# Down products of a gated feed-forward kernel moved: one wait for all chunks, and half of one group's products behind two steps of the next

## The reference

```python
x = x + L0_ffn(L0_cond(x))                  # shared + routed experts, top 2 of 8
# second layer
H     = x @ W.T                             # 256 -> 256
delta = ((x @ A_b.T) @ B_b.T) * s_b         # rank 16, one adapter for each batch row
h     = H + delta
gate  = gelu(fp8(h) @ fp8(w_gating[0]))     # 256 -> 1024, bf16 out
up    =      fp8(h) @ fp8(w_gating[1])      # 256 -> 1024, bf16 out
out   = fp8(gate * up) @ fp8(w_linear)      # 1024 -> 256
x = x + out
```

## Time and profile before

| | |
|---|---|
| median of 3 runs | 429.93 us |
| profiled execution, its own time | 429.1 us |
| its span | 427.3 us |
| TensorE busy | 412.4 us (97%) |
| VectorE, ScalarE, GpSimd busy | 309.2, 249.0, 193.2 us |
| groups 0 to 6 of the second layer | 289 to 411.7 us, some 17.5 us each |
| last group to the end | 411.7 to 427.3 us |

### The profile page before, as it was taken

The page is one execution under the profiler, slowest core; times in us unless marked ns, Lnnn a source line. Parts: engine busy times, 40 slices in busy tenths (PEclk is TensorE's granted clock), DMA queues, the critical chain, the costliest instruction groups (busy, mean ns, idle before and its releaser), DMA issues.

```text
span 427.3 us, 8683 instructions
## 1 busy us (share of the span) xinstructions
PE 412.4 (97%) x2954; PEld 331.7 (78%) x2954; DVE 309.2 (72%) x728; ACT 249.0 (58%) x552; POOL 193.2 (45%) x198
## 2 busy tenths in 40 slices
PE   7999789999999999999999999999999999999996
PEld 5567578887889999999999998885665756657553
DVE  5987898997987666666666663759587786777845
ACT  2987544667335665556655654438475494664854
POOL 2404229900544544455445403646575575754020
PEclk9999999999999999999999999999999999999999
DMA  8998300000145554655555622321143232322111
GB/s 250 381 388 297 99 0 2 1 2 0 54 128 179 167 161 144 181 160 158 165 159 176 152 87 74 88 74 51 52 134 95 66 111 74 113 87 61 49 51 50
DMA packets 37290, 50.44 MB, mean 118 GB/s; under 512 B 4504, under 2 KB 30496, under 8 KB 37248
## 3 DMA queue, kind: packets, MB, share of 16 engines
q1 hardware_dynamic: 29600, 31.53, 21.8%
q0 software_dynamic: 6512, 17.71, 15.7%
q10 hardware_dynamic: 1136, 0.65, 0.6%
HBM read 32.18 MB, written 17.69 MB: 117 GB/s over the span
## 4 chain that ended last, share of the span: by engine, by line
PE 81%; ACT 8%; DVE 7%; issue 2%; DMA 2%; POOL 0%; DVEq 0%; ACTq 0%; POOLq 0%
PE bank L1132 16%; PE bank L1134 16%; PE bank L1133 15%; PE bank L1408 13%; PE bank L1423 6%; PE bank L1294 4%; ACT xtr L468 2%; PE bank L1333 2%; PE bank L1332 2%; PE bank L1314 2%; PE bank L1374 2%; ACT xtT L482 2%; PE bank L1222 1%; DVE hsf L761 1%; DMA pick<-in_pick 1%
## 5 line engine op out<-in xcount | busy, mean ns | idle before, releaser
L403 POOL DMA_INDIRECT xg<-kept,perm x71 | 68.1, 959 | 91.2 <-PE bank L1294 54.9
L1408 PE MATMUL bank<-h,wg 128*128 128x512 fp8e4 x256 | 61.6, 380 | 0.2 <-ACT ff L642 0.2
L1132 PE MATMUL bank<-w13h,xgl 128*128 x142 | 48.9, 344 | 0.4 <-issue 0.4
L1408 PEld LDWEIGHTS bank<-h,wg 128*128 128x128 fp8e4 x256 | 22.2, 98 | 33.9 <-ACT ff L642 13.3
L410 POOL DMA_INDIRECT ga<-slots_out,slot x32 | 32.8, 1026 | 33.3 <-SPq L349 17.3
L963 DVE TENSOR_TENSOR hrl<-bank,hrh 128x256 fp32r<-128x256 f32 (+1 forms) x36 | 15.1, 421 | 44.2 <-issue 36.5
L1134 PE MATMUL bank<-w13h,xgh 128*128 x142 | 45.5, 320 | 0.0
L1133 PE MATMUL bank<-w13l,xgh 128*128 x142 | 45.5, 320 | 0.0
L640 ACT ACTIVATE gel<-bank 128x512 bf16<-128x512 f32 x64 | 40.2, 627 | 6.4 <-PE bank L1408 3.2
L410 POOL DMA_INDIRECT gb<-slots_out,slot x32 | 37.7, 1178 | 9.8 <-issue 9.8
L642 ACT ACTIVATE ff<-bank 128x512 bf16<-128x512 f32 x64 | 40.6, 635 | 0.0
(11 more groups left out here) (199 smaller groups left out, 1167.8 us busy)
## 6 DMA issues: line engine op xcount, KB each, us to landing
slots_out<-yr SPq DMA_DIRECT2D x35, 256.0 KB
xres<-in_x SPq DMA_DIRECT2D x7, 512.0 KB, 10.3
kept<-xtr SPq DMA_DIRECT2D x7, 512.0 KB, 7.4
out_x<-fin SPq DMA_DIRECT2D x7, 512.0 KB
w13raw<-in_rw SPq DMA_DIRECT2D x8, 352.0 KB, 4.3
w2raw<-in_rw SPq DMA_DIRECT2D x8, 256.0 KB, 5.6
wgst<-in_wgate SPq DMA_DIRECT2D x16, 128.0 KB
xg<-kept,perm POOLq DMA_INDIRECT x71
```

The source lines that it names most:

```text
L403: pool.indirect_dma_start(out=xg[:, i % 2, j, :], out_offset=None, in_=kept, in_offset=bass.IndirectOffsetOnAxis(perm[:, 2 * i + j:2 * i + ...
L1132: pe.matmul(dst, al, bh, start=first, stop=False, skip_group_check=True)
L1408: ins = pe.matmul(bank[bk][:, :], wg8[:, kk, half, c * P:(c + 1) * P], h8[:, k, kk, :], start=(kk == 0), stop=(kk == KC - 1))
```

## The change

Three edits, all in the second layer:

```diff
 # ScalarE
                 for c in range(HC):
                     gelu(g, c, first)
+                    if c == 1 and last:
+                        down_out(g - 1, 1)
...
                 down_out(g, 0, first)
-                down_out(g, 1, first)
+                if g + 2 < GROUPS:
+                    down_out(g, 1, first)
 # TensorE
                 for c in range(HC):
                     ffn_up(g, k, c, first)
+                    if c == 1 and last:
+                        ffn_down(g - 1, 1, False, range(HC // 2, HC))
...
-                ffn_down(g, 0, first, range(2, 5))
+                ffn_down(g, 0, first, range(2, HC))
                 adapters_down(g + 1)
                 linear(g + 1, 0)
-                ffn_down(g, 0, first, range(5, HC))
                 linear(g + 1, 1)
                 adapters_up(g + 1)
-                ffn_down(g, 1, first)
+                ffn_down(g, 1, first, range(HC if g + 2 < GROUPS else HC // 2))
```

## The result

The changed kernel takes 451.57 us (median of 5 runs, 450.22 to 453.57) against 429.85 us before (5 runs, 429.12 to 430.27). The ratio is 1.0512, 95% interval 1.0479 to 1.0545: slower by 5.1%, 21.7 us. I had forecast 447.9 us and a range of 446.3 to 449.4. The direction and the place were right; the time lies outside the range, by a cost that I had set to zero.

What follows compares the result with a forecast made beforehand. TensorE, 81% of the span, was taken to bound the kernel. The median of 429.93 us plus 17.96 us for groups 0 to 6, with 0 for the moved half and the clock, gave 447.9 us, range 446.3 to 449.4.

Steps and rivals of the forecast that it cites:

- The wait: TensorE ahead of the merged down products, groups 0 to 6: idle 2.76 us each until chunk 7's fp8 cast.
- The sum of the waits: Groups 0 to 6 together: 2 x 2.63 + 5 x 2.54 = 17.96 us slower.
- The cover of the mask and the low part: Second linear stage and adapters' second stage: inputs ready about 0.5 us before use, cost 0.
- The moved half: Group 6's half behind two up steps of group 7: 0.82 us earlier start spent on ScalarE, net 0.
- The clock: TensorE's granted clock behind the new waits: stays full, no loss taken.
- the fourth rival: Clock falls to 1.2 GHz behind each wait, twelve products take twice as long: 9.2 us more, 457.1 us; chance 5%.
- Chunk by chunk issue: Merged down call: waits not merged, products start per chunk, 1.1 us less waiting per group, 440.2 us; chance 2%.
- The wait is not paid: Ahead of the twelve products: chunk 7's cast ready in time, only removed stalls count, 428.6 us; chance 2%.

Runs made afterwards that it cites:

- the products behind the linear stages: Kernel before, with the six products of chunks 5 to 7 moved behind the adapters' second stage in groups 0 to 6: 429.35 us, ratio 0.9993.
- the merged call alone: Kernel before, with one down call for chunks 2 to 7 in groups 0 to 6, group 6's second half left whole: 450.56 us, ratio 1.0503.
- the waits filled: Changed kernel plus 23 matmuls, results read by nobody, ahead of the wait in each of groups 0 to 6: 446.45 us, ratio 1.0413.
- the kernel with two waits: Changed kernel, its twelve products issued in the same place by two calls, chunks 2 to 4 then 5 to 7: 448.65 us, ratio 1.0453.

## Why the prediction was wrong, step by step

**The wait: right.** I worked out an idle time of 2.76 us in each group; the profile shows 2.54 in the first and 2.60 in the rest. What counts is the group's length: +2.54 worked out, 20.02 - 17.51 = +2.51 measured where the clock stayed up. That TensorE is held ahead of work that does not need chunk 7 is shown by the products behind the linear stages (no loss) and by the merged call alone (all of the loss).

**The sum of the waits: 5% high.** 17.96 us forecast; 17.05 with the waits filled. In the profiled executions groups 1 to 5 grow by 2.5 us each. The rest of the difference lies within the 1.5 us over which the runs of the filled kernel spread, and I haven't split it. This error of 0.9 us hid a part of the next one: the forecast of the loss was 17.96 and the measured loss 21.72, 3.8 us more.

**The cover of the mask and the low part: right.** I had about 0.5 us left at the adapters' second stage; it is 350.40 - 349.94 = 0.46.

**The moved half: right.** 0 forecast, ratio 0.9998 measured. In the changed kernel the Gelu of chunk 2 of the last group starts 3.30 us behind the first up matmul (438.83 and 435.53), against 2.60 before (414.28 and 411.68); I had 3.49. The up matmuls' lead is spent there. From that Gelu to the end of the span it is 13.0 us in both kernels.

**The clock: the step that failed.** The prediction says "I take no loss, since the nearest row shows none", and it gave the fourth rival, a fall behind every wait, 5%. The term is 4 to 5 us in the median instead of 0: the distance from 446.45 to the 450.6 and 451.6 of the unfilled kernels. Idle stretches of 1.9 and of 2.6 us bring the half rate in some groups and not in others (four of seven in the profiled executions of the kernel with two waits and of the whole change, two of seven with the merged call alone). My other reason, that TensorE is busy for 17 us between two waits, did not protect it either. The prediction's own sign of being wrong, a granted clock that leaves 1.00 behind the waits, is what the profile shows.

The row that I leaned on the earlier trace rows was one wait of 2.09 us at the start, and I misread it. It doesn't show a full clock behind the wait. The trace of the kernel before holds no record of the granted clock for the first 11.92 us of its span, and the 1.00 of rows 8 is printed where nothing is recorded. The matmuls tell the level. Eleven of the same form stand a little behind that wait in both traces; in that of the changed kernel, shown second, the record begins earlier, at 9.44:

```profile
5.87 2.53 PE L1179 MATMUL bank<-onesb 128*128 128x128 bf16 x22
...
9.41 1.35 PE L1179 MATMUL bank<-onesb 128*128 128x128 bf16 x11
```

```profile
9.30 0.84 PE L1182 MATMUL bank<-onesb 128*128 128x128 bf16 x11
```

They take 1.35 us ahead of the recorded part and 0.84 where almost all of them lie within it. The 22 right behind the wait go at the slow pace too, 2.53 us, or 0.11 each, which is what a down product of twice the columns takes at full clock. So TensorE was at the half rate there, and the row said nothing on whether a wait of 2 us is harmless to a full clock.

The fourth rival itself had the price wrong as well, 9.2 us. It doubled the twelve products in all seven groups, while the falls came in some of the groups and cost 1.4 to 1.6 us each in the whole change and with two waits. A fall of 3.41 us isn't tied to the twelve products: in group 3 it covers them (364.43 to 367.84), in group 0 it begins 1.2 us behind the wait (302.99) and most of it lies on the linear stage. The Trainium skill (TensorE: Matmul & The Clock Gate, "Why this matters for your kernels") warns of idle gaps between bursts; here the trace agrees with the direction of it, and falls came behind gaps shorter than the one it names. Not shown by any run is what makes one group fall and the next not.

**Rivals that fell.** Chunk by chunk issue would have given 440.2; the wait was one, of 2.6 us. "The wait is not paid" (428.6) fell with the same seven waits.

## What to carry to other kernels

A helper that waits once for the last operand of its range turns two calls into one long wait when they are merged: look up what stands behind the new wait in the engine's list, and when the operand is ready by the trace. Where TensorE is dense, price an idle stretch of 1.9 us or more, the shortest behind which the clock fell here, with a chance of the half rate, and put such a cost into the range even if one row of the trace seems to show none. Before you call such a row harmless, check by the pace of its matmuls that the clock was full ahead of the wait. Stalls of 0.1 to 0.2 us that repeat in a loop can be filled with work that is ready, which earned 1.3 us here.

## What I had not expected of the hardware

- The clock fell behind idle stretches of 1.9 us at least as readily as behind 2.6 us: 6 us lost against 4 to 5. Behind 1.3 us it fell in none of five runs; with 3.5 us it fell in all seven groups of the profiled execution.
- A fall can begin while TensorE is still idle or when it is busy again. In the whole change, group 3, it begins at 364.43, 0.5 us ahead of the end of the wait. In the kernel with two waits it comes late: in group 2 the wait ends at 339.27 and the clock is still full until about 340.4, when TensorE has been busy again for 1 us: the stretch of 340 to 341 shows 0.71.
- A fall lasts 3.4 us with waits of 1.9 and 2.6 us (5 us at a mean of 0.66 for the former), and 6.8 us in four of the seven groups with waits of 3.5.
- Each of the twelve profiled executions begins at the half rate, by the pace of those 22 matmuls (2.52 to 2.53 us in all twelve), and the printed clock doesn't tell: its record begins 9.0 to 12.0 us into the span, and the stretches ahead of it show 1.00.
- Matmuls whose results nobody reads make a kernel with such waits 4 to 6 us faster.
